# A recurrence's chunk of sixteen tokens, solved in two halves of eight

## The reference, cut to what matters

```python
def step(S, inp):
    qt, kt, vt, at, bt = inp
    err = jnp.einsum('bhij,bhj->bhi', S, kt) - vt
    S = at[..., None] * S - bt[..., None, None] * (err[..., None] * kt[:, :, None, :])
    o = jnp.einsum('bhij,bhj->bhi', S, qt)
    return (S, o)
```

## Time and profile before

| | before |
|---|---|
| median of three runs | 7530.25 us |
| profiled execution, device time | 7518.62 us |
| its span | 7516.8 us |
| DVE busy | 5944.7 us (79%) |
| POOL busy | 4502.3 us (60%) |
| PE busy | 4968.9 us (66%) |
| ACT busy | 4111.2 us (55%) |
| mean granted TensorE clock | 0.765 |

### The profile page before, as it was taken

How to read it: one execution, slowest core, us unless ns; L and a number is a source line. 1 busy time by engine, 2 the same in 40 slices (tenths; PEclk the granted TensorE clock), 3 DMA queues, 4 the chain that set the end, 5 groups by cost and what they waited for, 6 DMA issues and landing times. The chain is left out here.

```text
span 7516.8 us, 144745 instructions
## 1 busy us (share of the span) xinstructions
PE 4968.9 (66%) x42311; PEld 3150.7 (42%) x42311; DVE 5944.7 (79%) x15810; ACT 4111.2 (55%) x10434; POOL 4502.3 (60%) x3976
## 2 busy tenths in 40 slices
PE   5556656565665666656666534777777777777777
PEld 3444444444444444444444422334333333433343
DVE  6999999999999999999999984556665566665665
ACT  5666666666666666666666642444444444444444
POOL 4999999999999999999999992111111111111110
PEclk7777777777677677777677766888888888888888
DMA  3545554554555455455445531111111111111111
GB/s 99 135 118 117 137 125 116 128 135 115 119 135 123 114 135 130 116 123 136 118 117 136 121 89 49 48 46 46 48 46 44 42 42 42 43 44 42 42 42 35
DMA packets 953132, 684.14 MB, mean 91 GB/s; under 512 B 836659, under 2 KB 888531, under 8 KB 938196
## 3 DMA queue, kind: packets, MB, share of 16 engines
q1 hardware_dynamic: 653524, 516.82, 28.5%
q10 hardware_dynamic: 299008, 159.92, 8.9%
HBM read 423.47 MB, written 253.17 MB: 90 GB/s over the span
## 5 line engine op out<-in xcount | busy, mean ns | idle before, releaser
L397 POOL TENSOR_TENSOR qp<-qp,ab 128x1024 f32<-128x1024 f32 (+15 forms) x1024 | 1411.9, 1379 | 80.4
L1154 POOL TENSOR_TENSOR ot<-ot,ln_w 128x1024 f32<-128x1024 f32 x64 | 150.6, 2354 | 1408.7 <-ACT ot L1429 1408.7
L1573 DVE TENSOR_REDUCE nmax<-w_bank 128x1 f32<-128x512 f32 x1024 | 637.8, 682 | 326.2 <-PE w_bank L1199 317.6
L718 DVE SCALAR_TENSOR_TENSOR p_bank<-y,conv_w,p_bank 128x128 f32<-128x128 f32 x3072 | 832.5, 345 | 65.9 <-ACT p_bank L549 38.5
L406 POOL TENSOR_TENSOR qp<-qp,pt 128x832 f32<-128x832 f32 (+7 forms) x512 | 810.7, 1583 | 40.1
L438 PE MATMUL d_bank<-xd,kt 32*64 32x128 f32 x7936 | 402.5, 361 | 555.1 <-DVE st L736 548.4
L504 PE MATMUL p_bank<-xnT,wqkv 128*128 128x128 f32 x4096 | 581.5, 307 | 215.4 <-ACT st L562 175.2
L504 PE MATMUL rows_bank<-xnT,wqkv 128*128 128x128 f32 x2048 | 375.6, 368 | 503.6 <-DVE eb L818 503.6
L811 DVE TENSOR_TENSOR rows_bank<-rows_bank,t 128x960 f32<-128x960 f32 (+14 forms) x960 | 671.5, 699 | 33.1
L807 DVE TENSOR_TENSOR rows_bank<-rows_bank,ab 128x960 f32<-128x960 f32 (+14 forms) x960 | 661.1, 689 | 0.0
L504 PEld LDWEIGHTS p_bank<-xnT,wqkv 128*128 128x128 f32 x4096 | 552.9, 219 | 244.9 <-issue 244.9
(11 more groups left out here) (203 smaller groups left out, 11629.1 us busy)
## 6 DMA issues: line engine op xcount, KB each, us to landing
decay_or_prod<-decay_dram SPq DMA_DIRECT2D x124, 1024.0 KB, 11.1
prod_dram<-decay_or_prod ACTq DMA_DIRECT2D x64, 1280.0 KB, 10.4
kp<-prod_dram SPq DMA_DIRECT2D x64, 640.0 KB, 6.6
qp<-prod_dram SPq DMA_DIRECT2D x64, 640.0 KB, 14.0
a_dram<-at ACTq DMA_DIRECT2D x64, 512.0 KB
v_dram<-vt ACTq DMA_DIRECT2D x64, 512.0 KB
vb<-v_dram SPq DMA_DIRECT2D x64, 512.0 KB, 4.0
ab<-a_dram SPq DMA_DIRECT2D x64, 512.0 KB, 8.8
```

Of the source, the lines that this page charges most:

```text
L397: link(nc.gpsimd.tensor_tensor(q, q, ab[:, g, r:r + 1, :].to_broadcast([128, w, DV]), ALU.mult), 0 if shared else 1)
L718: nc.vector.scalar_tensor_tensor(out=zz, in0=y[:, m, :, tap:tap + C], scalar=conv_w[:, m, tap:tap + 1], in1=zz, op0=ALU.mult, op1=ALU.add) ...
L1573: nc.vector.tensor_reduce(nmax[:, n:n + 1], bank[:], AX.X, ALU.max, negate=True).then_inc(freed, 1)
```

## The change

The chunk is solved in two halves of eight tokens. In each half DVE works on widths 7 to 0 instead of 15 to 0 (`half` takes the place of `solve`); for the last three widths the outer product and the sum are one instruction per row. What the first half's updates give the keys and queries of the second half is summed by TensorE: `scores` multiplies keys with later keys and queries on PE and ACT masks them into `sc`; after the first half, its eight scaled updates go to memory (`e_dram`) and come back in eight loads as `xe`, `cross` makes 64 matmuls of 32x32 with 64 columns, ACT evicts them to `xo` and writes them (`x_dram`), and SP loads them as `xk`. DVE adds `xk` at the start of the second half, POOL adds it to the queries. POOL's and ACT's widths are halved in the same way, and POOL scales the values for the step ahead.

The order of every engine is written anew. On PE, `project` 5, `gates` and `betas` now stand behind update pair 0, and `cross` stands ahead of pairs 1 to 3; `products` stands ahead of `front2`. On SP, `upd_dram` is written after the loads of `vb` and `kp` of the next step, and the loads of `qp` and `db` stand ahead of the loads of `xd`, which come first in the next slot. The convolution's banks are three that take turns. The loop starts one slot earlier.

The diff, cut to its core (eight columns of indentation left out):

```diff
 def conv_bank(j):
-    if j // 2 == 1:
-        return rows_bank[:, C // 2 * (j - 2):C // 2 * (j - 1), :].rearrange("p r i -> p (r i)")
-    return p_bank[j % 2][:]
+    return (p_bank[0], p_bank[1], c_bank)[j % 3][:]
 
...
     def slot(s, n, g, lo, hi):
...
-        if updates(lo - 1, hi - 1):
-            t = s - 1
-            sp.wait_ge(solve_chain, SOLVE_OPS * (t + 1))
-            held(sp, sp_passed)
-            if due(dma_of(xd_in, n, g, -3, 16 * GB)[1]):
-                sp.wait_ge(*dma_of(xd_in, n, g, -3, 16 * GB))
-                held(sp, sp_passed)
-            sp.dma_start(upd_dram[o].rearrange("b h t i -> (b h) (t i)"), eb[:]).then_inc(upd_wr[o], 16)
-        if valid(lo, hi):
-            src = prod_dram[g].rearrange("m (h k r) c -> (m h) k r c", h=4, k=2)
-            sp.wait_ge(*dma_of(p_wr, n, g, 0))
-            held(sp, sp_passed)
-            if due(SOLVE_OPS * s):
-                sp.wait_ge(solve_chain, SOLVE_OPS * s)
-                held(sp, sp_passed)
-            sp.dma_start(kp[:], src[:, 0]).then_inc(kp_in[g], 16)
         if updates(lo - 1, hi - 1):
             t = s - 1
             sp.wait_ge(*dma_of(upd_wr, n, g, -1))
@@ -304,32 +311,26 @@
             for b in range(GB):
                 sp.dma_start(xd[C * b:C * b + C, :, b % 2, :],
                              upd_dram[o][b].rearrange("h t i -> t h i")).then_inc(xd_in[o], 16)
-        if updates(lo - 1, hi - 1):
...
+            if due(s + 3):
+                sp.wait_ge(xn_ready, s + 3)
+            held(sp, sp_passed)
+            load_x(n + 1 + g, o)
...
+        if valid(lo, hi):
+            sp.wait_ge(solve_chain, SOLVE_OPS * s + FIRST_HALF_OPS)
             held(sp, sp_passed)
-            dst = o_dram.rearrange("(n t) b h i -> n t b h i", t=C)[:, :, GB * o:GB * o + GB]
-            sp.dma_start(dst[bass.ds(n - 1 + g, 1)].rearrange("o t b h i -> (o b h) t i"), qp[:, o, :, 0:DV]).then_inc(o_wr[o], 16)
+            if due(dma_of(xe_in, n, g, -2, 16 * GB)[1]):
+                sp.wait_ge(*dma_of(xe_in, n, g, -2, 16 * GB))
+                held(sp, sp_passed)
+            sp.dma_start(e_dram[g].rearrange("b h t i -> (b h) t i"), eb[:, 0:HALF]).then_inc(e_wr[g], 16)
+            sp.wait_ge(*dma_of(v_wr, n, g, 0))
+            held(sp, sp_passed)
+            sp.wait_ge(*dma_of(e_wr, n, g, 0))
+            held(sp, sp_passed)
+            for b in range(GB):
+                sp.dma_start(xe[C * b:C * b + HALF].rearrange("t (h i) -> t h i", h=H),
+                             e_dram[g][b].rearrange("h t i -> t h i")).then_inc(xe_in[g], 16)
+            sp.wait_ge(*dma_of(x_wr, n, g, 0))
+            held(sp, sp_passed)
+            sp.dma_start(xk[:], x_dram[g].rearrange("t b h i -> (b h) t i")).then_inc(xk_in[g], 16)
+        if valid(lo + 1, hi + 1):
+            src = prod_dram[o].rearrange("m (h k r) c -> (m h) k r c", h=4, k=2)
+            sp.wait_ge(*dma_of(v_wr, n, g, 1))
+            held(sp, sp_passed)
+            sp.dma_start(vb[:, o], v_dram[o].rearrange("t b h i -> (b h) t i")).then_inc(vb_in[o], 16)
+            sp.wait_ge(*dma_of(p_wr, n, g, 1))
+            held(sp, sp_passed)
+            if due(SOLVE_OPS * s):
+                sp.wait_ge(solve_chain, SOLVE_OPS * s + solved(HALF))
+                held(sp, sp_passed)
+            elif valid(lo, hi):
+                sp.wait_ge(solve_chain, solved(HALF))
+                held(sp, sp_passed)
+            sp.dma_start(kp[:], src[:, 0]).then_inc(kp_in[o], 16)
+        if updates(lo, hi):
+            sp.wait_ge(solve_chain, SOLVE_OPS * (s + 1))
+            held(sp, sp_passed)
+            if due(dma_of(xd_in, n, g, -2, 16 * GB)[1]):
+                sp.wait_ge(*dma_of(xd_in, n, g, -2, 16 * GB))
+                held(sp, sp_passed)
+            sp.dma_start(upd_dram[g].rearrange("b h t i -> (b h) (t i)"), eb[:]).then_inc(upd_wr[g], 16)
+        if valid(lo + 1, hi + 1):
+            if due(dma_of(o_wr, n, g, -1)[1]):
+                sp.wait_ge(*dma_of(o_wr, n, g, -1))
+                held(sp, sp_passed)
+            sp.dma_start(qp[:, o], src[:, 1]).then_inc(qp_in[o], 16)
+        if updates(lo, hi):
+
+            sp.wait_ge(*dma_of(dec_wr, n, g, 0))
+            held(sp, sp_passed)
+            for par in range(2):
+                rows = decay_dram[g][par:par + 1].to_broadcast([64, GB * HP, DV])
+                sp.dma_start(db[64 * par:64 * par + 64], rows).then_inc(db_in[g], 16)
...
+
+        pool.wait_ge(*dma_of(kp_in, n, g, 0))
+        first = acs[:, 0:1].to_broadcast([128, HALF, DV])
+        held(pool, pool_passed)
+        link(nc.gpsimd.tensor_tensor(kp[:, HALF:C, 0:DV], kp[:, HALF:C, 0:DV], first, ALU.mult), 1)
         pool.wait_ge(*dma_of(qp_in, n, g, 0))
+        held(pool, pool_passed)
+        link(nc.gpsimd.tensor_tensor(qp[:, g, HALF:C, 0:DV], qp[:, g, HALF:C, 0:DV], first, ALU.mult), 1)
...
+            if r == HALF:
+                pool.wait_ge(*dma_of(xk_in, n, g, 0))
+                rest = qp[:, g, HALF:C, 0:DV]
+                held(pool, pool_passed)
+                link(nc.gpsimd.tensor_tensor(rest, rest, xk[:, HALF:C], ALU.add))
...
+    def cross(s, n, g):
+
+        pe.wait_ge(*dma_of(xe_in, n, g, 0, 16 * GB))
+        for u in range(2):
+            bank = use(cross_use(s), u)
+            held(pe, pe_passed)
+            for k in range(HP):
+                h = HP * u + k
+                for q in range(4):
+                    mm = nc.tensor.matmul(bank[32 * q:32 * q + 32, DV * k:DV * k + DV],
+                                          sc[32 * q:32 * q + 32, h % 2, h // 2, :],
+                                          xe[32 * q:32 * q + 32, DV * h:DV * h + DV], start=True, stop=True)
+            mm.then_inc(f_filled, 1)
...
     def slot(s, n, g, lo, hi):
-        if valid(lo + 1, hi + 1):
-            for j in range(2, CONV_BANKS):
+        front, ahead, state = valid(lo + 1, hi + 1), valid(lo + 2, hi + 2), updates(lo - 1, hi - 1)
+        before = s - 1, n - 1 + g, 1 - g
+        if front:
+            for j in range(2, CONV_BANKS - 1):
                 project(s + 1, 1 - g, j)
-        if updates(lo - 1, hi - 1):
-            update(s - 1, n - 1 + g, 1 - g, (0,))
-        if valid(lo + 2, hi + 2):
+        if state:
+            update(*before, (0,))
+        if front:
+            project(s + 1, 1 - g, CONV_BANKS - 1)
+        if ahead:
             gates(s + 2, g)
-        if updates(lo - 1, hi - 1):
-            update(s - 1, n - 1 + g, 1 - g, (1, 2, 3))
-        if valid(lo + 2, hi + 2):
             betas(s + 2, g)
-        if valid(lo + 1, hi + 1):
+        if valid(lo, hi):
+            cross(s, n, g)
+        if state:
+            update(*before, (1, 2, 3))
+        if front:
+            scores(s + 1, 1 - g)
+            products(s + 1, n + g, 1 - g)
             front2(s + 1, n + g, 1 - g)
-            products(s + 1, n + g, 1 - g)
-        if valid(lo + 2, hi + 2):
+        if ahead:
             for j in range(2):
                 project(s + 2, g, j)
 
...
+    def crossed(s, n, g, state):
+
+        if state:
+            act.wait_ge(decayed, s)
+        if due(dma_of(x_wr, n, g, -1)[1]):
+            act.wait_ge(*dma_of(x_wr, n, g, -1))
+        for u in range(2):
+            bank = filled(cross_use(s), u)
+            nc.scalar.activation(xo[:, 512 * u:512 * u + 512], bank[:], ACT.Copy).then_inc(f_freed, 1)
+        act.wait_ge(f_freed, cross_use(s) + 2)
+        if due(dma_of(xk_in, n, g, -2)[1]):
+            act.wait_ge(*dma_of(xk_in, n, g, -2))
+        act.dma_start(x_dram[g].rearrange("t b h i -> b t (h i)"), xo).then_inc(x_wr[g], 16)
 
     def shares(s, n, g, tokens):
...
     def slot(s, n, g, lo, hi):
-        if valid(lo + 1, hi + 1):
+        front, ahead, state = valid(lo + 1, hi + 1), valid(lo + 2, hi + 2), updates(lo - 1, hi - 1)
+        if front:
             for j in range(2, CONV_BANKS):
                 evict(s + 1, 1 - g, j)
-                silu(s + 1, 1 - g, j - 2)
-        if valid(lo + 2, hi + 2):
+                if j < CONV_BANKS - 1:
+                    silu(s + 1, 1 - g, j - 2)
+        if ahead:
             transposed(s + 2, g)
-        if valid(lo + 1, hi + 1):
-            silu(s + 1, 1 - g, CONV_BANKS - 2)
+            gates(s + 2, n + 1, g)
+            betas(s + 2, n + 1, g)
         if valid(lo, hi):
-            seed_rows(s, n, g, valid(lo + 1, hi + 1))
-        if valid(lo + 1, hi + 1):
-            silu(s + 1, 1 - g, CONV_BANKS - 1)
+            shares(s, n, g, SHARED[:2])
+        if front:
+            silu(s + 1, 1 - g, 3)
             place_keys(s + 1, 1 - g)
-        if valid(lo + 2, hi + 2):
-            gates(s + 2, n + 1, g)
         if valid(lo, hi):
-            shares(s, n, g, FIRST_SHARES)
-        if valid(lo + 2, hi + 2):
-            betas(s + 2, n + 1, g)
-        if valid(lo + 1, hi + 1):
+            crossed(s, n, g, state)
+        if front:
+            silu(s + 1, 1 - g, 4)
+            masked_scores(s + 1, 1 - g)
+            silu(s + 1, 1 - g, 5)
```

(92 more changed lines are left out.)

236 lines of the change are left out of this document (121 added, 115 removed).

## The result

| | before | after |
|---|---|---|
| median of four runs | 7527.27 us | 7960.86 us |
| span of the profiled execution | 7516.8 us | 7965.2 us |
| DVE busy | 5944.7 us | 5336.3 us |
| POOL busy | 4502.3 us | 3049.4 us |
| mean granted TensorE clock | 0.765 | 0.750 |

The ratio is 1.057, with an interval of 1.055 to 1.059: slower. The forecast was 8035 us, the range 7400 to 8450. DVE and POOL lost over 600 and 1400 us of work, and the time grew by 434.

The account below looks back on a forecast made before the run. The data's circle through memory, from v_dram landed to the same moment a step later, was taken as the bound: terms summed to 77.8 us a step against 69.5, so 7518.6 + 62 x 8.3 = 8033, called 8035 us; range 7400 to 8450.

Parts of the forecast that it names:

- (a): SP's queue, from v_dram landed through vb, kp, upd, qp and db to xd landed: 26.0 us, bounds 17.2 and 26.9.
- second rival: SP's queue lets xd pass db: 69.0 us a step, 7488 us, a little faster or the same; chance 0.12.
- (b): PE, once xd has landed: update pair 0 at 1.1 us and project 5 at 2.0, together 3.1.
- (c): ACT evicts project 5's bank, 2.2 us, then the transposes, 0.5: reached at 31.8 us.
- (d): Gates 10.4 us and betas 0.6, no longer hidden beside DVE's work: reached at 42.8 us.
- (e): cross on PE, 64 matmuls or 128 records at 22 ns: 2.8 us, or 7.9 at 62 ns.
- fourth rival: Worse: cross at 62 ns a record, v fully behind prod, xd at 26.9: 87 us a step, 8600 us; chance 0.07.
- (f): Update pairs 1 to 3, each 2.0 us on PE and 1.3 on DVE, one after the other: 9.9 us.
- (g): scores from the issue of pair 3, 2.8 us, then four small evictions and a SiLU: reached at 58.6 us.
- (h): Products with their evictions: 7.1 us, reached at 65.7 us.
- (i): prod issued in 0.4 us, landing after 10.7; v behind it in ACT's queue adds 1.0: circle closes at 77.8 us.
- first rival: Faster: the way through memory is covered, the step runs through the first half, 64.6 us, 7215 us; chance 0.15.

Follow-up runs that it names:

- e2: Changed kernel with project 5, gates and betas put ahead of update pair 0 on PE: 7692.5 us.
- e1: Changed kernel with SP issuing the two db loads right behind the eight xd loads, not ahead of them: 7812.2 us.
- e6: e2 with ACT doing SiLU 0 and 1 ahead of eviction 3 and SiLU 2 ahead of eviction 4: 7860.9 us.
- e7: e2 with both the SP order of e5 and the ACT order of e6: 7514.4 us.
- e9: e7 with the values computed and sent ahead of the products, DVE's last taps ahead of the second pair of states: 7513.6 us.
- e10: e9 with ACT issuing the writes of the values and of the gates behind the masked scores: 7253.3 us.
- e12: e7 with only the gates' write (a_dram) issued later on ACT, behind the masked scores: 7351.2 us.
- e4: Changed kernel without the e_dram and xe transfers and their waits, so its result is wrong: 7927.0 us in one run.
- e5: e2 with the outputs, ab, nb, x and the decay's write moved behind the xe loads in SP's queue: 7659.1 us.
- e3: Changed kernel with both edits, xd ahead of db on SP and project 5, gates and betas ahead of pair 0 on PE: 7768.2 us.

## Why the prediction was right

The direction, the mechanism and the size held, and the time is 0.9% under the forecast: 76.2 us a step over the whole recurrence where 77.8 were worked out. That it came so close is in part luck: the terms missed by up to 2.4 us, in both directions, and nearly cancel. Measured times are means over the steps from 600 to 4200 us, from the vb issue that K releases.

- **(a) xd**: pair 0 starts at 24.4, predicted 26.0. The choice of the high side was right: all of db is there at 21.8 and all of xd at 24.2, so xd did not pass db, and the second rival falls; that completion is "not FIFO per issuing engine", as the Trainium skill has it (DMA: Bandwidth & Descriptors, Queues, rings and completion order), did not help xd here. The sign that the prediction named, a landing over 8 us after issue, holds for the median of the eight loads, 10.9. It compared this with the last load, though, and that one lands 7.6 us after its issue, before the change 4.8. Much of the delay comes ahead of that, in the issuing, which takes 10.7 us instead of 3.8; the prediction had no term for it.
- **(b) pair 0 and project 5**: 5.5, predicted 3.1. This was mis-sized. In the step shown PE needs 1.98 and 3.57 us for what the earlier trace rows have as 1.10 and 2.02. The stretches of PE in the changed kernel, where the third number from the end is the granted clock, tell why:

```profile
2035.20:2037.10 1.90, 1.87 (x32) 1.61 (x32) 1.61 (x5) 0.00 (x0) 0.00 (x0) 0.50 0.93 213
2037.20:2040.50 3.30, 3.30 (x19) 3.30 (x17) 3.30 (x11) 0.00 (x0) 0.00 (x0) 0.52 0.67 186
2043.50:2046.80 3.30, 3.30 (x4) 0.91 (x4) 3.17 (x9) 1.13 (x1) 0.00 (x0) 0.54 0.17 38
2048.10:2050.00 1.90, 1.90 (x6) 0.66 (x5) 0.53 (x3) 0.60 (x1) 0.00 (x0) 1.00 0.00 0
```

PE stood idle for 8 us and comes out of it at 0.50, the 1.2 GHz level; at 2048 it is back at 1.00, 2.4 GHz, and four gate matmuls take 1.98 instead of 3.49. A wait on PE costs its length and some of the work behind it again. The price stood in the earlier trace rows: a pair there took 1.98 us behind a wait of 2.75, and (b) took the 1.10 of a pair that had waited for 0.60 only.
- **(c), (d)**: 12.1 to the start of cross (29.9 to 42.0), predicted 13.7. Cross starts at 42.0, predicted 42.8. That nothing hides the gates any more was right, and e2, which hides them again, gains 268 us.
- **(e) cross**: 2.3, predicted 2.8. The choice of 22 ns a record over 62 was right: 2.25 / 128 is 18 ns. The fourth rival falls with it. It holds for a PE that comes to cross from its own work, at 0.98: in e1, e6, e7, e9, e10 and e12, where PE waits for xe first, the clock over cross is 0.51 to 0.55 and cross takes 3.5 to 4.3 us.
- **(f)** pairs 1 to 3: 9.1 (states end at 53.4), predicted 9.9.
- **(g), (h)** scores to the issue of prod: 12.5, predicted 10.2. The sum took PE's work alone. In the timeline PE stands inside the scores for 4.63 us with the mark "issue", and from 500 to 4800 us such waits are 126.3 us in 55 places, 2.3 us a step, which is as much as the term was short. The kernel has no wait inside the scores, and the stop comes at the same place in nearly every step, behind the 92nd matmul record for one group and the 123rd for the other. No run was aimed at it, and its cause stays open.
- **(i)**: from prod's issue at 65.9 to the next K at 76.6 it is 10.7, predicted 12.1. prod lands in 7.7 instead of 10.7 us, and v takes 7.6 from its own issue at 69.1 instead of 6.3; so v's landing is the later one by itself, where the prediction had it 1.0 behind prod.

In sum -1.6 + 2.4 - 1.6 - 0.5 - 0.8 + 2.3 - 1.4 = -1.2, which is 76.6 - 77.8.

Of the side paths, xk was right: the second half starts at 62.3, predicted 61.8, and is through 14.6 us later, at about K. SP's longest wait is the sign that failed: 1387.5 us on x_dram against 1014.9 on v_dram, where v_dram was expected first. SP stands for x_dram from the end of the xe loads on, and that wait costs nothing by itself; the two are in one queue and share a step between them. On the path of e two errors cancel: the first half starts at 12.9 and not at 8.8, but e then has less ahead of it and lands at 30.3, predicted 32. The last xe is issued at 33.3, the prediction had it landed at 39, and e4 shows that this path did not decide.

DVE's saving was priced at 10.7 us a step and is 65.6 - 56.0 = 9.6. Scaling in pieces of 512 was priced 1.0 too high (0.69 us each, so 2.07 for three, as one of 1024 took before), the second half's sum of 448 too low (1.70 us). None of it is on the circle. It is the answer to where the saving went: into DVE's waits, 526.8 us for PE and 499.4 us for xk in 56 steps; 76.2 - 56.0 = 20.2 us a step are idle, of which the prediction had 19.

The first rival, memory way covered, at 64.6 us a step and 7215 us, is wrong for this change. e10, in which xe releases cross, has 65.1 and 7253, but that its number fits so well is luck. From the issue of kp to the end of the first half e10 needs 21.2 us (the rival: 15.9), from there to cross 7.3 (9.8), for cross 3.8 (2.8) and from there to the next kp 32.8 (36.1), and in e10 the values go ahead of the products, so vb's load is not on the circle. What the rival lacked is that xd need not be early if PE does not wait for it; its condition, xd by K + 12.8, was put for the order of PE as it stands in the change.

## What to carry to other kernels

When work is handed through memory inside a step, price the circle of the data and not the engine that is relieved, and ask of each in-order engine what stands behind the instruction that waits for the late transfer: moving two lines was worth 268 us here, and 598 in the best version. Then see to the big transfers that nobody needs soon: they belong behind the short round trips that somebody waits for, across queues too. Edits of this kind are to be tried together, since a single one can move a transfer into another's way: the SiLUs' edit lost 168 us on e2 (e6) and gained 145 on e5 (e7). Moving xd ahead of db lost on e2 (e3) and was not tried with the rest in place.
